# New homes in SBUF for the buffers of a windowed attention and gated FFN kernel, and one pair of loads moved

## What is computed

```python
xn = layernorm(x)
q, k, v = xn @ wq, xn @ wk, xn @ wv          # 32, 8 and 8 heads of 128
q, k = rope(q), rope(k)
scores = (q . k) * 128 ** -0.5               # causal, window of 128
s = (softmax(scores) @ v) @ wo
a, b = xn @ W1.T, xn @ W3.T                  # W1, W3, W2 unpacked from 4 bits and scaled
g = silu((silu(a) * b) @ W2.T)
out = x + s * g
```

## Time and profile before

| | |
|---|---|
| median of 3 runs | 804.82 us |
| the profiled execution | 804.47 us |
| its span, first to last instruction | 802.7 us |
| TensorE busy | 797.4 us (99% of the span) |
| VectorE busy | 568.1 us (71%) |
| GpSimd busy | 473.6 us (59%) |
| ScalarE busy | 428.7 us (53%) |
| DMA, mean over the span | 67 GB/s |

### The profile page before, as it was taken

How to read it: one execution, slowest core, us unless ns; L and a number is a source line. 1 busy time by engine, 2 the same in 40 slices (tenths; PEclk the granted TensorE clock), 3 DMA queues, 4 the chain that set the end, 5 groups by cost and what they waited for, 6 DMA issues and landing times.

```text
span 802.7 us, 13468 instructions
## 1 busy us (share of the span) xinstructions
PE 797.4 (99%) x3966; PEld 671.7 (84%) x3966; DVE 568.1 (71%) x1637; ACT 428.7 (53%) x1104; POOL 473.6 (59%) x355
## 2 busy tenths in 40 slices
PE   8999999999999999999999999999999999999998
PEld 7888888888888888888888888888888888888887
DVE  7625868577448867777786777778677767867785
ACT  5412313223138685666666566666656666665672
POOL 1102324224246875767487576748757674878997
PEclk9999999999999999999999999999999999999999
DMA  9549625211000400400040040004004000420102
GB/s 281 176 163 276 143 78 154 63 46 53 1 27 14 132 14 1 127 6 13 2 131 13 0 129 2 13 0 131 13 0 127 3 13 0 131 65 0 40 0 106
DMA packets 51908, 54.00 MB, mean 67 GB/s; under 512 B 4128, under 2 KB 33184, under 8 KB 51872
## 3 DMA queue, kind: packets, MB, share of 16 engines
q1 hardware_dynamic: 51728, 53.50, 22.3%
q10 hardware_dynamic: 144, 0.07, 0.0%
HBM read 47.25 MB, written 6.29 MB: 67 GB/s over the span
## 4 chain that ended last, share of the span: by engine, by line
PE 92%; POOL 4%; issue 2%; DVE 1%; ACT 1%; DMA 0%; POOLq 0%; ACTq 0%
PE bank L1329 26%; PE bank L1330 26%; PE bank L1331 26%; PE bank L1512 3%; PE bank L1528 3%; PE bank L1545 2%; PE bank L1546 2%; PE bank L1547 2%; PE bank L1554 1%; POOL swap L448 1%; PE bank L1551 1%; PE bank L1552 1%; POOL acc L479 1%; POOL q L452 1%; POOL ph L471 1%
## 5 line engine op out<-in xcount | busy, mean ns | idle before, releaser
L448 POOL TENSOR_TENSOR swap<-swap,cst 128x512 f32<-128x512 f32 x80 | 108.3, 1354 | 41.6 <-ACT swap L692 41.6
L713 ACT ACTIVATE probs<-probs,nmx 128x128 f32<-128x128 f32 x256 | 100.0, 392 | 60.1 <-DVE nmx L1103 60.0
L1329 PE MATMUL bank<-xh,wih 128*128 128x512 f32 x320 | 128.9, 403 | 0.0
L1330 PE MATMUL bank<-xl,wih 128*128 128x512 f32 x320 | 125.1, 391 | 0.0
L1331 PE MATMUL bank<-xh,wil 128*128 128x512 f32 x320 | 125.0, 391 | 0.0
L1329 PE MATMUL bank<-woh,oh 128*128 128x512 f32 (+1 forms) x260 | 101.0, 389 | 0.0
L1330 PE MATMUL bank<-wol,oh 128*128 128x512 f32 (+1 forms) x260 | 100.5, 387 | 0.0
L1331 PE MATMUL bank<-woh,ol 128*128 128x512 f32 (+1 forms) x260 | 100.5, 387 | 0.0
L399 POOL TENSOR_TENSOR hl<-act_h,hh 128x512 fp32r<-128x512 f32 x22 | 32.0, 1453 | 99.9 <-ACT hh L594 99.9
L452 POOL TENSOR_TENSOR q<-q,swap 128x512 f32<-128x512 f32 x64 | 86.1, 1345 | 6.7 <-DVE q L1078 1.8
L471 POOL TENSOR_TENSOR ph<-ph,cst 128x512 fp32r<-128x512 f32 x32 | 41.9, 1310 | 73.3 <-ACT ph L728 73.3
(11 more groups left out here) (137 smaller groups left out, 2025.2 us busy)
## 6 DMA issues: line engine op xcount, KB each, us to landing
raw<-in_wq SPq DMA_DIRECT2D x32, 256.0 KB, 4.8
raw<-in_wo SPq DMA_DIRECT2D x32, 256.0 KB, 4.9
pk<-in_w SPq DMA_DIRECT2D x44, 128.0 KB, 3.8
sc<-in_s SPq DMA_DIRECT2D x44, 128.0 KB, 3.8
vals<-stage SPq DMA_DIRECT2D x16, 256.0 KB, 2.2
vraw<-vals SPq DMA_DIRECT2D x16, 256.0 KB, 2.9
pk<-in_w SPq DMA_DIRECT2D x11, 256.0 KB, 2.7
sc<-in_s SPq DMA_DIRECT2D x11, 256.0 KB, 3.1
```

The costliest lines, as they stand in the source:

```text
L448: nc.gpsimd.tensor_tensor(v, v, spread(sin.unsqueeze(1), P, 2, SEQ), ALU.mult).then_inc(sin_done, 1)
L713: e = nc.scalar.activation(probs[:, s, c0:c1], probs[:, s, c0:c1], ACT.Exp, bias=nmx[:, s, i:i + 1], scale=-1.0, accum_out=rsum[:, s, i:i ...
L1329: nc.tensor.matmul(out_, sh, mh, start=(i == 0), stop=False)
L1330: nc.tensor.matmul(out_, sh, ml, start=False, stop=False)
```

## The change

**New homes.** These are the addresses in bytes within a partition of the main buffers in the two built programs, and what is left of them after division by 128:

| buffers | before | after | rest by 128, before | after |
|---|---|---|---|---|
| `cst` (rotation, masks; before also `ident`) | 32896 | 32896 | 0 | 0 |
| `ident` (before in `cst`) | 36992 | 125056 | 0 | 0 |
| `wih`, `wil` | 55936, 66176 | 65664, 55424 | 0, 0 | 0, 0 |
| `W13h`, `W13l` (after: `fh`, `fl`) | 109184, 117376 | 75904, 84096 | 0, 0 | 0, 0 |
| `xh`, `xl` | 76416, 92800 | 92288, 108672 | 0, 0 | 0, 0 |
| `wvh`, `wvl` | 185920, 202304 | 126016, 142400 | 64, 64 | 64, 64 |
| `W2h`, `W2l` | 202304, 214592 | 146496, 216128 | 64, 64 | 64, 64 |
| `hh`, `hl` | 169536, 185920 | 183360, 199744 | 64, 64 | 64, 64 |
| `xn` | 169536 | 183360 | 64 | 64 |
| `k`, `q` | 113280, 125568 | 134208, 138304 | 0, 0 | 64, 64 |
| `kh`, `kl`, `qh`, `ql` (after in `fh`, `fl`) | 117376 to 137856 | 75904 to 88192 | 0 | 0 |
| `probs` | 141952 | 158784 | 0 | 64 |
| `vh`, `vl` | 154240, 158336 | 166976, 171072 | 0, 0 | 64, 64 |
| `ph`, `pl` | 162688, 168832 | 146496, 152640 | 0, 0 | 64, 64 |
| `oh`, `ol` | 174976, 191360 | 191552, 199744 | 0, 0 | 64, 64 |
| `woh`, `wol` | 183168, 199552 | 183360, 175168 | 0, 0 | 64, 64 |

The 64 comes from the small buffers. `shc`, `warm`, `stat`, `mv`, `std` and the 512 bytes of `idle` (before) or `ident` (after) take 960 bytes together, 7 x 128 + 64. Before they lie within `ffn`, behind what the attention uses of it, and move only `xn`, `wvh`, `wvl`, `hh`, `hl`, `W2h`, `W2l`; after they lie ahead of every scope, and move all that follows. `early` is now under `ffn`'s first buffers, so that `pk2` and `sc2` share space with `wvh`, and `W2` shares it with `q`. Loops, shapes and the order of TensorE, ScalarE and GpSimd are the same.

```diff
--- before.py
+++ after.py
@@ -66,72 +66,76 @@
         gate = sb("gate", [P, NT, D], f32)
-        cst = sb("cst", [P, C_W], f32)
+        cst = sb("cst", [P, C_ID], f32)
         cos, sin = cst[:, C_COS:C_COS + SEQ], cst[:, C_SIN:C_SIN + SEQ]
         causal, plain, far, keep = [cst[:, C_MASK + n * P:C_MASK + (n + 1) * P] for n in range(4)]
-        ident = cst[:, C_ID:C_ID + P]
         raw = sb("raw", [P, RING, D], f32)
+        wil = sb("wil", [P, 5, DT, P], f32r)
         wih = sb("wih", [P, 5, DT, P], f32r)
-        wil = sb("wil", [P, 5, DT, P], f32r)
+
+        fh = sb("fh", [P, 4 * PK], f32r)
+        fl = sb("fl", [P, 4 * PK], f32r)
+        W13h, W13l = [f[:, :].rearrange("p (s m t n) -> p s m t n", s=2, m=2, t=DT) for f in (fh, fl)]
+        kh, kl = [f[:, 0:2 * PK].rearrange("p (b n) -> p b n", b=2) for f in (fh, fl)]
+        qh, ql = [f[:, 2 * PK:4 * PK].rearrange("p (h b n) -> p h b n", h=GH, b=2) for f in (fh, fl)]
         xh = sb("xh", [P, DT, TOK], f32r)
         xl = sb("xl", [P, DT, TOK], f32r)
+        ident = sb("ident", [P, P], f32)[:, :]
+        shc = sb("shc", [P, 6], i32)
+        warm = sb("warm", [P, 4], f32)
+        stat = sb("stat", [P, NT, 6], f32)
+        mv = sb("mv", [P, NT, 2], f32)
+        std = sb("std", [P, 4, NT], f32)
+
         main = ctx.enter_context(ExitStack())
+        early = ctx.enter_context(ExitStack())
+        wvh = sb("wvh", [P, 2, DT, VH], f32r, early)
+        wvl = sb("wvl", [P, 2, DT, VH], f32r, early)
+        sb("under_w13", [P, 6 * PK * 2], f32, early)
+        xn = sb("xn", [P, NT, D], f32, early)
+        sb("under_hl", [P, 4 * TOK], f32, early)
+        stage = sb("stage", [P, 4, VH], f32, early)
+        idle = stage[:, 3, 0:P]
+        early.close()
         ffn = ctx.enter_context(ExitStack())
-        W13h = sb("W13h", [P, 2, 2, DT, P], f32r, ffn)
-        W13l = sb("W13l", [P, 2, 2, DT, P], f32r, ffn)
-        pk = sb("pk", [P, 2, 2, PK], i32, ffn)
-        sc = sb("sc", [P, 2, 2, PK], f32, ffn)
-        nib = sb("nib", [P, 2, PK], i32, ffn)
-        W13 = sb("W13", [P, 2, PK], f32, ffn)
         act_h = sb("act_h", [P, 2, IT], f32, ffn)
         pk2 = sb("pk2", [P, 2, D], i32, ffn)
         sc2 = sb("sc2", [P, 2, D], f32, ffn)
         nib2 = sb("nib2", [P, D], i32, ffn)
         W2 = sb("W2", [P, 2, D], f32, ffn)
-        shc = sb("shc", [P, 6], i32, ffn)
-        warm = sb("warm", [P, 4], f32, ffn)
-        idle = sb("idle", [P, P], f32, ffn)
-        stat = sb("stat", [P, NT, 6], f32, ffn)
-        mv = sb("mv", [P, NT, 2], f32, ffn)
-        std = sb("std", [P, 4, NT], f32, ffn)
-        early = ffn.enter_context(ExitStack())
-        xn = sb("xn", [P, NT, D], f32, early)
-        wvh = sb("wvh", [P, 2, DT, VH], f32r, early)
-        wvl = sb("wvl", [P, 2, DT, VH], f32r, early)
-        stage = sb("stage", [P, 4, VH], f32, early)
-        early.close()
+        sb("under_q", [P, D], f32, ffn)
+        W2h = sb("W2h", [P, W2R, D], f32r, ffn)
+        pk = sb("pk", [P, 2, 2, PK], i32, ffn)
+        sc = sb("sc", [P, 2, 2, PK], f32, ffn)
+        nib = sb("nib", [P, 2, PK], i32, ffn)
+        W13 = sb("W13", [P, 2, PK], f32, ffn)
         hh = sb("hh", [P, 4, TOK], f32r, ffn)
         hl = sb("hl", [P, 4, TOK], f32r, ffn)
-        W2h = sb("W2h", [P, W2R, D], f32r, ffn)
         W2l = sb("W2l", [P, W2R, D], f32r, ffn)
         ffn.close()
+        vraw = sb("vraw", [P, 2, IT // P, HD], f32, main)
         swap = sb("swap", [P, 2, IT], f32, main)
         k = sb("k", [P, 2, IT], f32, main)
-        kh = sb("kh", [P, 2, IT], f32r, main)
-        kl = sb("kl", [P, 2, IT], f32r, main)
         q = sb("q", [P, GH, IT], f32, main)
-        qh = sb("qh", [P, GH, 2, P], f32r, main)
-        ql = sb("ql", [P, GH, 2, P], f32r, main)
+        ph = sb("ph", [P, 3, GH * P], f32r, main)
+        pl = sb("pl", [P, 3, GH * P], f32r, main)
         probs = sb("probs", [P, 2 * GH, 2 * P], f32, main)
-        vraw = sb("vraw", [P, 2, IT // P, HD], f32, main)
         vh = sb("vh", [P, 2, IT // P, HD], f32r, main)
         vl = sb("vl", [P, 2, IT // P, HD], f32r, main)
+        wol = sb("wol", [P, GH, D], f32r, main)
+        woh = sb("woh", [P, GH, D], f32r, main)
+        oh = sb("oh", [P, 4, GH, P], f32r, main)
+        ol = sb("ol", [P, 4, GH, P], f32r, main)
+        acc = sb("acc", [P, NT, D], f32, main)
         pace = sb("pace", [P, 4 * GH], f32, main)
         nmx = sb("nmx", [P, 2 * GH, 2], f32, main)
         rsum = sb("rsum", [P, 2 * GH, 2], f32, main)
         rinv = sb("rinv", [P, 2 * GH, 2], f32, main)
-        ph = sb("ph", [P, 3, GH * P], f32r, main)
-        pl = sb("pl", [P, 3, GH * P], f32r, main)
-        oh = sb("oh", [P, 4, GH, P], f32r, main)
-        woh = sb("woh", [P, GH, D], f32r, main)
-        ol = sb("ol", [P, 4, GH, P], f32r, main)
-        wol = sb("wol", [P, GH, D], f32r, main)
-        acc = sb("acc", [P, NT, D], f32, main)
         bank = [ctx.enter_context(nc.psum_tensor(f"bank{i}", [P, 512], f32)) for i in range(8)]
         S_B, PJ_B, T_B, O_B = bank[0:2], bank[2:4], bank[4:6], bank[6:8]
@@ -304,9 +308,9 @@
                 keep_v(n)
             load13(2, 0)
             load13(2, 1)
-            load2(0)
             for n in range(VU // 2, VU):
                 keep_v(n)
+            load2(0)
             sp.dma_start(cst[:, 0:C_ID], const[:, 0:C_ID]).then_inc(const_in, 16)
             def load_in(slot, g, c):
@@ -410,7 +414,7 @@
                 nc.gpsimd.tensor_tensor(wvl[:, half, d, :], raw[:, s, :], wvh[:, half, d, :].bitcast(f32),
                                         ALU.subtract).then_inc(wvl_first, 1)
-            nc.gpsimd.memset(idle[:, :], 0.0).then_inc(idle_set, 1)
+            nc.gpsimd.memset(idle, 0.0).then_inc(idle_set, 1)
             pool.wait_ge(xn_here, 1)
             wv_lo(0, 0)
             wv_lo(0, 1)
@@ -1182,6 +1186,7 @@
             ffn_add(FT // 2 - 1, range(6, NT))
             kq_lo(0, 0, 0)
             kq_lo(0, 0, 1)
+            dve.wait_ge(W2l_done, FT)
             cos_part(0, 0, 2)
             ffn_add(FT // 2, range(4))
             v_lo(0, 0)
@@ -1447,7 +1452,7 @@
             def keep_busy(n):
                 for _ in range(n):
-                    nc.tensor.matmul(bank[5][:, 0:P], idle[:, :], idle[:, :], start=True, stop=True)
+                    nc.tensor.matmul(bank[5][:, 0:P], idle, idle, start=True, stop=True)
             def w13_tile(t):
                 for half in range(2):
```

## The result

The changed kernel takes 806.77 us (median of 9 runs, 806.57 to 807.08), the kernel before 804.63 us on the same chips (9 runs, 804.40 to 804.96): a ratio of **1.0028, 95% interval 1.0019 to 1.0037**. It is slower by 2.1 us, 0.28%, past the 0.2% line that the prediction drew (the interval begins just under it), and so on the side to which the prediction gave 0.38, against 0.58 for no difference. The forecast was 806.3 us and a range of 803.5 to 808.0.

What follows compares the result with a forecast made beforehand. It took TensorE's intervals between product starts as the bound. Value units 0, attention 0.39 + 0.52 + 0.6 = 1.5 us, loads and wait 0, other engines 0: 804.82 + 1.5 = 806.3 us, range 803.5 to 808.0.

Steps and rivals of the forecast that it cites:

- What bounds the kernel: TensorE, busy 797.4 of 802.7 us, waits 2.1 us: time is 3966 products times the interval between their starts.
- What sorts the cases: TensorE's running operand and weights loaded meanwhile: unequal address rests by 128 cost 0.013 or 0.037 us once, 6.7 ns a product lasting.
- Value units: 0: 192 products with `wvh` against `xh`: rests stay 64 and 0, so they keep 233.3 ns; cost 0.
- Known switches: 0.91 us: Attention: projection to attend or output projection 30 x 0.013 = 0.39 us, attend back to projection 14 x 0.037 = 0.52 us.
- Entries from scores: Score products (`kh` 0) into attend or output projection (64): about 45 mismatches at 0.013, 0.6 us; bounds 0 to 1.7.
- Score units: Inside 128 score units, 256 mismatches between `k`/`qh` and `kh`/`q`: 0 to 1.7 us possible, 0 taken.
- the slower rival: Score units fall out of step: 256 mismatches at 6.7 ns, 45 entries at 0.037 us; 809.1 us; chance 10%.
- "I allow 0.5 us" for a gain: Inside score units, a start that falls into step could gain; 0.5 us allowed, 0 taken.
- Turns of probabilities: 0: Turns with `ident` at 0 and `probs` at 64, the pair turns of `x` had before: 0.
- Moved loads and wait: 0: `load2(0)` behind the stores has 13 us to spare; VectorE's `W2l_done` semaphore is 20 us old by then: 0.
- nearness: Rival: operand distance counts, so value units fall to 226.7 ns, giving back 1.3 us: 803.5 us; chance 13%.
- Placement counting for nothing: Rival: value units slow for another reason, switch losses come from semaphores; 804.8 us; chance 15%.

Runs made afterwards that it cites:

- the run with 192 bytes: Kernel before with `wvh`, `wvl` and `stage` 192 bytes later; only the value units' interval was read: 22.30 / 96 = 232.3 ns.
- after_all0: Changed kernel with 64 unused bytes ahead of every scope, so `wvh` and all that follows have rest 0 like `xh`: 803.24 us, ratio 0.9981 to the kernel before.
- v0_far: Kernel before with 64 unused bytes ahead of `wvh`, so `wvh`, `wvl`, `stage` have rest 0, still 107 KB behind `xh`: 803.75 us, ratio 0.9989.

## Why the prediction was right, and where its steps were off

- **What bounds the kernel.** Right. No wait to speak of came or went; the 2.2 us are in the intervals between TensorE's starts, and 64 unused bytes bring them about or take them away.
- **What sorts the cases.** The idea was right, the number wrong. I took the rest by 128, since all rests in the trace of before were 0 or 64 by it. The buffers of before are equally well sorted by 256, and the run with 192 bytes tells the two apart: equal by 128, unequal by 256, 232.3 ns. In this change both rules give the same forecast, so the step failed without harm.
- **Value units: 0.** Right: 233.3 ns, though `wvh` now lies 33 KB from `xh` (the prediction says 34; by the addresses it is 33,728 bytes, and its 107 KB counts KB of 1024).
- **Known switches: 0.91 us** (0.39 to attend and the output projection, 0.52 back). Measured 0.35 and 0.57, and 0.12 for the three products behind the output projection, which I had set at 0: 1.04 us.
- **Entries from scores: 0.6 us taken, 0 to 1.7 allowed.** Mis-sized: 1.29 us. I took the 13 ns of a switch to attend for 45 entries; there are 46, and into attend each costs 45 ns and into the output projection 20 on average (9 to 43). By the traces these runs begin out of step already before the change (233 and 231 ns behind scores into attend), and in the changed kernel all nine products stay out of step (241, 235, 233, 236, 224, 231, 236, 228 and 233 ns).
- **Score units: 0 taken, 0 to 1.7 allowed.** Measured 0.22 us, 1.8 ns a unit, well short of the 13 ns that the slower rival needed. What fills the 0.20 us behind `k`, which the prediction calls the drain of a float32 product, no run shows. That rival's other half did largely come: the entries cost 28 ns on average, and it priced them at 37.
- **"I allow 0.5 us" for a gain.** It came, but elsewhere: -0.53 us in projections behind scores, whose own operands are matched. The run with `k` and `q` alone off makes them its likely cause, and gives 12 of the 18 ns.
- **Turns of probabilities: 0.** Measured +0.11 us in the projections behind them.
- **Moved loads and wait: 0.** Right; tried alone they give a ratio of 0.9999.
- **The sum.** 1.5 us forecast, 2.1 us measured (2.27 us between the traces). The forecast came as near as it did with some luck: the entries cost 0.7 us more than taken, and the terms set at 0 (0.12, 0.22 and 0.11 us) and the -0.53 us that it had only allowed for cancelled one another. With the entries at their measured 1.29 us the sum would have been 2.2.

Of the rivals, nearness is excluded by two runs. Placement counting for nothing is excluded by every run in which 64 bytes moved the time. The page of the Trainium skill cited there ("TensorE: Matmul & The Clock Gate", section "Step-by-step: what each phase is for") says that loading the next weights takes nothing from the running matmul; by the 233.3 and 226.7 ns that a shift of 64 bytes switches between, here the load costs 6 to 7 ns a product or nothing, depending on the addresses. Why 256 bytes is the period stays open: the runs show the addresses to be the cause, not the circuit behind it. Why the two signs of a step cost 13 and 40 ns stays open too.

## What to carry to other kernels

In a kernel like this one, which TensorE bounds with one load of weights for each 128 x 512 float32r product, give all buffers that it reads the same address modulo 256, the running ones and the loaded ones. It is worth 1.4 to 1.5 us of 804.7 here, 0.2%, and other shapes and types were not tried by themselves. A few small buffers of odd size ahead of a scope can undo that for everything behind them. To find such a loss, don't read the busy share: divide a long stretch of starts by the number of products and compare stretches of one shape. And look at the addresses of the built program before believing a layout to be neutral.

## What the runs showed of the hardware that was not expected

- A 128 x 512 float32r product with its own 128 x 128 weights takes 226.7 ns in a stream if the running operand and the weights loaded meanwhile have the same address modulo 256 bytes, and 232.3 to 233.3 ns if not (tried at -64, -32, +32 and 128 bytes).
- A single unmatched switch throws a matched stream out of step for 3 products (12 to 13 ns in all) if the weights being loaded lie 64 bytes below the running operand modulo 256, and for 10 to 11 (about 40 ns) if they lie 64 above.
- Distance in SBUF doesn't matter: matched operands ran at 226.7 ns at 33 KB (`after_all0`) and at 107 KB (`v0_far`).
